# A planner with its first transfers in the order of use and newly searched rank lists: a two-layer conditioned transformer on one Trainium2 core

## What is computed

```python
ada = (silu(cond) @ Wada.T + bada).reshape(8, 1, 6, 256)
gamma1, gamma2, scale1, scale2, shift1, shift2 = [ada[:, :, i, :] for i in range(6)]
x = x + attn0(ln(x) * (scale1 + 1) + shift1) * gamma1        # 16 heads of 16, cosine-normed q and k
x = x + (gelu((ln(x) * (scale2 + 1) + shift2) @ Wfc1.T + bfc1) @ Wfc2.T + bfc2) * gamma2
h = rms(x) * ln1_w * (1 + cond @ tw1.T)
x = x + attn1(rope(h @ Wq.T), rope(h @ Wk.T), h @ Wv.T) @ Wo.T     # 8 query heads of 32, one k/v head
h = rms(x) * ln2_w * (1 + cond @ tw2.T)
x = x + (silu(h @ Wg.T) * (h @ Wu.T)) @ Wd.T
```

## Time and profile before

| what | value |
|---|---|
| three runs | 308.78, 309.8, 311.77 us; median 309.8 us |
| profiled execution | 313.7 us, of which the span from first to last instruction is 311.6 us |
| mean granted TensorE clock | 0.967 of full |
| PE busy | 291.3 us of the span (93%), `warm` products included |
| DVE, ACT, POOL busy | 215.4, 205.5, 153.9 us |

### The profile page before, as it was taken

How to read it: one execution, slowest core, us unless ns; L and a number is a source line. 1 busy time by engine, 2 the same in 40 slices (tenths; PEclk the granted TensorE clock), 3 DMA queues, 4 the chain that set the end, 5 groups by cost and what they waited for, 6 DMA issues and landing times.

```text
span 311.6 us, 7095 instructions
## 1 busy us (share of the span) xinstructions
PE 291.3 (93%) x2412; PEld 244.5 (78%) x2412; DVE 215.4 (69%) x527; ACT 205.5 (66%) x698; POOL 153.9 (49%) x289
## 2 busy tenths in 40 slices
PE   7999979898879989978999999999999999999996
PEld 7879767666757768865987787899888988888985
DVE  4884599979496999988859787576445875463431
ACT  3574399999975998987889865737772342662210
POOL 3658687385976955797424456521424321222000
PEclk9795899999986999999999999999999999999999
DMA  6999532002010010000002000000000000000000
GB/s 185 243 299 331 150 104 97 8 1 70 0 36 0 16 54 3 1 3 0 2 0 69 1 3 0 2 2 17 18 3 2 0 8 28 1 2 25 12 2 34
DMA packets 14035, 14.28 MB, mean 46 GB/s; under 512 B 1568, under 2 KB 12960, under 8 KB 14000
## 3 DMA queue, kind: packets, MB, share of 16 engines
q1 hardware_dynamic: 14000, 13.83, 14.7%
HBM read 12.76 MB, written 1.06 MB: 44 GB/s over the span
## 4 chain that ended last, share of the span: by engine, by line
PE 56%; DVE 19%; POOL 12%; issue 6%; ACT 4%; DMA 1%; SPq 1%; DVEq 0%; POOLq 0%
PE ps_shared L1570 16%; PE ps_shared L1377 8%; PE ps_shared L1379 7%; PE ps_shared L1378 7%; PE ps_shared L1543 4%; DVE z L1265 3%; PE ps_output L1524 2%; PE ps_shared L1508 2%; ACT z L990 2%; PE ps_scores L1497 2%; DVE neg_max L1276 2%; PE ps_scores L1407 2%; PE ps_shared L1413 2%; DMA X<-in_x 1%; PE ps_shared L1397 1%
## 5 line engine op out<-in xcount | busy, mean ns | idle before, releaser
L990 ACT ACTIVATE z<-z,neg_max 128x128 f32<-128x128 f32 x128 | 49.9, 404 | 5.8 <-DVE neg_max L1276 5.8
L830 POOL TENSOR_TENSOR h_lo<-xn,h_hi 128x256 fp32r<-128x256 f32 x32 | 24.1, 756 | 35.5 <-ACT h_hi L954 31.6
L1570 PE MATMUL ps_shared<-Wfc2T,g_h 128*128 128x256 f32 x128 | 33.0, 403 | 0.5 <-DVE g_h L1335 0.5
L1508 PE MATMUL ps_shared<-ident,z 128*128 128x128 f32 x192 | 29.4, 276 | 4.1 <-ACT z L990 1.9
L994 ACT ACTIVATE z<-ps_scores,neg_max 128x128 f32<-128x128 f32 x64 | 22.6, 368 | 14.7 <-DVE neg_max L1282 14.4
L1010 ACT ACTIVATE probsT<-ps_shared 128x512 f32<-128x512 f32 x48 | 28.8, 599 | 4.6 <-PE ps_shared L1508 3.6
L884 POOL TENSOR_TENSOR z<-z,row_inv 128x512 f32<-128x512 f32 x16 | 16.6, 1040 | 28.7 <-DVE row_inv L1290 28.5
L1570 PE MATMUL ps_shared<-WdT,g_h 128*128 128x256 f32 x128 | 30.1, 381 | 0.5 <-DVE g_h L1348 0.5
L1046 ACT ACTIVATE g_a<-ps_shared 128x256 f32<-128x256 f32 x32 | 12.4, 386 | 25.8 <-PE ps_shared L1379 21.4
L1508 PEld LDWEIGHTS ps_shared<-ident,z 128*128 128x128 f32 x192 | 22.0, 140 | 8.7 <-issue 6.3
L1570 PEld LDWEIGHTS ps_shared<-Wfc2T,g_h 128*128 128x128 f32 x128 | 24.2, 199 | 5.0 <-issue 1.0
(11 more groups left out here) (164 smaller groups left out, 884.7 us busy)
## 6 DMA issues: line engine op xcount, KB each, us to landing
gamma<-gamma_scratch SPq DMA_DIRECT2D x8, 256.0 KB, 3.6
stage<-in_Wada SPq DMA_DIRECT2D x6, 256.0 KB, 4.9
X<-in_x SPq DMA_DIRECT2D x4, 256.0 KB, 3.8
stage<-in_Wqkv SPq DMA_DIRECT2D x4, 256.0 KB, 5.5
Wfc2T<-in_Wfc SPq DMA_DIRECT2D x1, 1024.0 KB, 8.1
stage<-in_Wfc SPq DMA_DIRECT2D x4, 256.0 KB, 5.2
WdT<-in_Wd SPq DMA_DIRECT2D x1, 1024.0 KB, 6.7
stage<-in_Wg SPq DMA_DIRECT2D x4, 256.0 KB, 2.6
```

Source lines behind the costliest of these rows:

```text
L830: pool.tensor_tensor(h_lo[:, m, :, j * P:(j + 1) * P], h_full[:, m, j, :, :], h_hi[:, m, :, j * P:(j + 1) * P].bitcast(F32), ALU.subtract) ...
L990: ins = act.activation(z[:, d, u, :], z[:, d, u, :], ACT.Exp, bias=neg_max[:, d, u:u + 1], accum_out=head_sum[:, n % 2, t, u, b:b + 1])
L1508: ins = pe.transpose(bank[:, u * P:(u + 1) * P], z[:, G % DEEP, u, :], ident[:, :])
L1570: ins = pe.matmul(psum[b][:, 0:C], g_h[:, f, j * P:(j + 1) * P], WT1[name][:, f, :], start=(f == 0), stop=(f == FT - 1))
```

## The change

1. The ten first DMA steps get an order by hand (`FIRST`): their ranks are replaced by their places in that list, less a million. `pos` and `columns` are issued by ACT, ahead of its first instruction, and no longer by SP.
2. All rank lists (`GROUP_US`, `ATT_BASE`, `MLP_BASE`, `CHUNK_SHIFT`, `MLP_SPAN`, `SHIFT`) have new values.
3. Some planned durations are set anew, and `fc1` and `gate_up` may in the plan not run before the third-last gate is done. No instruction waits for more than before by it.
4. The clock model counts a `modulate` as 0.15 of its time, measures recent work over a sliding stretch when it decides on a `warm`, and keeps a high clock at a busy share of 0.6 (0.55 before).

No arithmetic, tile or semaphore of a step is changed; but all five orders, the banks and the number and places of the `warm` products come out of the planner anew.

```diff
+FIRST = ([("load_x", 0)] + [("load", c) for c in range(5)] + [("load_small",), ("load_x", 1), ("load", 5), ("load", 6),
+                                                              ("load_x", 2)])
...
-ATT_BASE = [-4247.0, -1474.0, -480.5, -362.5, 1970.0, -2902.0, 13.0, 1115.0]
-MLP_BASE = [936.0, 5182.0, -1432.5, 1460.0, -2095.0, -3629.5, 3064.0, -4297.5]
+ATT_BASE = [-4846.0, -3968.5, -278.0, -1190.0, 872.5, -4610.5, -4606.5, -699.0]
+MLP_BASE = [-999.0, 5454.0, -3139.0, 1474.0, -3599.0, -3395.0, 8429.5, -748.5]
...
-WARM_US, WARM_KEEP, WARM_RAISE = 0.22, 0.55, 0.95
+WARM_US, WARM_KEEP, WARM_RAISE = 0.22, 0.6, 0.95
+ACTIVITY = {"modulate": 0.15}
...
-    add(("cond_tanh",), "ACT", 2.8, at=-9)
+    add(("cond_tanh",), "ACT", 3.6, at=-9)
...
-        add(("load_x", p), "SP", 0.95, [],
+        add(("load_x", p), "SP", 0.95 if p else 1.7, [],
             at=-4.5 if p == 0 else ATT_BASE[2 * p - p % 2] + START - 20)
...
-                add(("qk_root", n), "Pool", 3.1, [("qk_sum", n)], at=a)
-                add(("qk_scale", n), "DVE", 0.75, [("qk_root", n)], at=a)
+                add(("qk_root", n), "Pool", 3.35, [("qk_sum", n)], at=a)
+                add(("qk_scale", n), "DVE", 0.95, [("qk_root", n)], at=a)
...
-            add(key, "PE", 1.51, [("norm_low", "m", 2 * r + 1), ("weight_low", w_ready)] + o[-1:], "shared", at=a)
+            add(key, "PE", 1.51, [("norm_low", "m", 2 * r + 1), ("weight_low", w_ready)] + o[-1:] + done[-3:-2], "shared", at=a)
...
-    return {k: (*v[:5], round(v[5] - path[k], 3)) for k, v in steps.items()}
+    return {k: (*v[:5], FIRST.index(k) - 1e6 if k in FIRST else round(v[5] - path[k], 3)) for k, v in steps.items()}
...
-                    us *= slow
-                    active += us
+                    us *= slow
+                    share = ACTIVITY.get(k[0], 1.0)
+                    active += us * share
+                    worked.append((now, now + us, share))
...
-                    if active < share * (now - window * CLOCK_WINDOW):
+                    since = now - CLOCK_WINDOW
+                    while worked and worked[0][1] <= since:
+                        worked.pop(0)
+                    recent = sum(w * (t1 - max(t0, since)) for t0, t1, w in worked)
+                    if recent < (WARM_KEEP if slow == 1.0 else WARM_RAISE) * min(now, CLOCK_WINDOW):
...
-            sp.dma_start(cols[:, 2 * N_SEQ:V0 + N_VEC], columns).then_inc(vec_loaded, 16)
-            sp.dma_start(pos_i[:, :], pos).then_inc(pos_loaded, 16)
...
         @block.scalar
         def _(act):
+            act.dma_start(cols[:, 2 * N_SEQ:V0 + N_VEC], columns).then_inc(vec_loaded, 16)
+            act.dma_start(pos_i[:, :], pos).then_inc(pos_loaded, 16)
```

More of the change, by code:

```diff
@@ L90 @@
+MLP_SPAN = [308.5, 2292.5]
 SHIFT = {
[L91 to L110, removed]
+    'warm': 900.0, 'angles': -2777.5, 'attn_copy': 1801.0, 'cond_silu': 3034.0, 'cond_tanh': 1647.0, 'down':
@@ new lines @@
+    4045.5, 'exp': 4489.0, 'fc1': -6047.5, 'gamma_load': -3148.0, 'gamma_store': 4661.0, 'gate': 3951.0,
+    'gate_up': 1799.5, 'gelu': -3728.5, 'gelu_in': 1876.0, 'gelu_inner': 1673.0, 'head_clip': -3201.5,
+    'head_exp': 2007.5, 'inv_copy': 2629.0, 'inv_spread': -1819.5, 'inv_turn': -3087.5, 'k_copy': 863.0,
+    'k_turn': 614.5, 'load': -2701.0, 'load_small': -2304.5, 'load_whole': 3744.0, 'load_x': -1760.5,
+    'mask_add': 437.0, 'modulate': 4093.5, 'modulated': -2328.0, 'norm_apply': -7684.5, 'norm_high':
@@ new lines @@
+    -4248.5, 'norm_low': 781.5, 'norm_mod': 1141.0, 'norm_probs': 963.0, 'norm_root': 11715.5, 'norm_stats':
+    -5932.5, 'norm_turn': 3032.5, 'probs_copy': -804.5, 'probs_turn': -897.0, 'project': -47.0, 'q_copy':
+    1206.0, 'q_turn': 3594.0, 'qk1_copy': 5525.5, 'qk1_turn': -10405.0, 'qk_copy': -2275.0, 'qk_high':
+    -2592.0, 'qk_low': -1220.5, 'qk_product': -4856.0, 'qk_root': 5555.0, 'qk_scale': 823.0, 'qk_square':
+    -4021.5, 'qk_sum': 919.5, 'qkv1_copy': -2814.5, 'qkv1_product': 3649.5, 'residual': -3156.0,
@@ new lines @@
+    'residual_add': 2346.5, 'rope': 6780.5, 'row_inverse': 3661.0, 'row_max': -4169.5, 'scores': 106.5,
+    'sines': 1611.5, 'store': 4409.0, 'sum_inverse': -6044.0, 'tanh': 3731.5, 'v_copy': -3365.0,
+    'v_product': -1368.0, 'values': -2796.5, 'weight_high': -579.5, 'weight_low': 2782.0, ('norm_stats',
+    'a'): -816.5, ('norm_stats', 'm'): 135.5, ('norm_root', 'a'): -619.5, ('norm_root', 'm'): -624.5,
+    ('norm_apply', 'a'): -3353.5, ('norm_apply', 'm'): 690.0, ('norm_turn', 'a'): -3449.0, ('norm_turn',
@@ L424, in make_orders, with clock @@
     plan, events, now, left = {}, [], 0.0, len(steps)
-    window, active, slow = 0, 0.0, 2.0
+    window, active, slow, worked = 0, 0.0, 2.0, []
+    def clock(now):
+        nonlocal window, active, slow
+        while now >= (window + 1) * CLOCK_WINDOW:
+            slow = 1.0 if active > 0.85 * CLOCK_WINDOW else 2.0 if active < 0.45 * CLOCK_WINDOW else slow
+            window, active = window + 1, 0.0
     warmed, n_pe = 0, sum(v[0] == "PE" for v in steps.values())
@@ L447, in make_orders @@
                 if e == "PE":
[L449 to L451 removed]
+                    clock(now)
                     us *= slow
[L453 removed]
+                    share = ACTIVITY.get(k[0], 1.0)
+                    active += us * share
+                    worked.append((now, now + us, share))
                 events.append((now + us, 0, k))
@@ L467, in make_orders @@
                         active += WARM_US * slow
+                        worked.append((now, now + WARM_US * slow, 1.0))
                         events.append((now + WARM_US * slow, 2, ("warm",)))
```

23 lines of the change are left out of this document (10 added, 13 removed).

## The result

The changed kernel takes 317.08 us (median of 4 runs, 316.31 to 317.96) against 310.5 us for the kernel before beside it: ratio 1.0211, 95% interval 1.0175 to 1.0246. It is slower by some 6.6 us, where 303.5 was forecast, in a range of 296 to 312.

A forecast was written before the change was run, and what follows sets the result against it. It saw a late start, a stretch nearly ACT's (40 to 88 us) and PE's block from 152 us. Terms 2.0 + 3.7 + 1.6 - 1.0 = 6.3 us, read from the profiled 313.7, taken off the median 309.8: 303.5, range 296 to 312.

The forecast's parts named there:

- First transfers: Start of the kernel: X of pair 0 loaded first brings the first `qk_product` forward, a gain of 2.0 us, lower end 0.
- `columns` and `pos` on ACT: Ahead of ACT's table load: `cond_tanh` some 0.8 us later, nothing on the path; without cover at most 0.8 us lost.
- The clock in the first 40 us: PE's chain from 24.22 us to `q_turn`: full clock removes its wait behind PE's queue, a gain of 3.7 us.
- the third stretch: Third low-clock stretch, 6.54 us of real work at half clock, 3.3 us too many; half taken as gain, 1.6 us.
- More `warm` products: PE before 40 us: 5 to 10 more pairs, half covered by waits, 1.0 us lost; ends 0 and 9.6 us.
- New ranks, planned durations and the gate condition: Reordering bounded by PE's idle 12.4 us from 40 to 152 us; entered as 0, ends +6 and -6 us.
- The slower one: Rival, PE's list from 14 to 34 us: added `warm` products stand before real work, 315.5 us; chance 0.13.
- The moved stretches: Rival: low-clock stretches move to new gaps between 40 and 152 us instead of going, 308.3 us; chance 0.28.
- the third rival: New lists also remove half of PE's 12.4 us idle from 40 to 152 us, 297.3 us; chance 0.17.
- The signs named in advance: Trace marks: right if first `exp` at 32 to 34 us; wrong if over 3 us at 0.50 after 14 us.

## Why the prediction was wrong, step by step

- *First transfers, 2.0 us.* X of pair 0 was issued at 0.71 us and there 2.9 us later, as said. The first product came at 12.88 us instead of 13.75: 0.9 us, at the low clock, so that the pass of six ended at 15.8, before at 15.4. The range of the term held this; its size was wrong. The weights came even earlier than priced (first `modulate` at 5.34 us, before at 7.88), but from there to the first product it took 7.5 us and not the 5.9 that I carried over. What I got wrong outright is the sentence that pair 1 "is wanted only by the second round's products". Who wants a tile is to be read from the list of the engine that reads it: pair 1's statistics stand on DVE ahead of pair 0's `norm_apply`. In the old lists that cost 4.8 us. In the changed ones the same wait is 2.04 us, at 14.00, and does no harm: the next step that PE needs, `qk_copy`, waits for PE until 15.85 anyway.
- *`columns` and `pos` on ACT, nothing on the path.* True for `modulate`; but `pos` landed 3.3 us after its issue (before, 1.9), the `angles` on DVE wait for it until 4.52 us, and `norm_stats` of pair 0, whose X was there by 3.6, stands behind them and runs at 5.78.
- *The clock in the first 40 us, 3.7 us, and the third stretch, 1.6 us.* In both, the changed kernel did not do what I expected: its plan puts in fewer `warm` steps, not more, and the clock fell in more places. The price itself holds for the execution from which it was read: the kernel before, held at full clock, takes 309.28 us, 4.4 less than the profiled 313.7, where the two terms came to 5.3. `q_turn` then ends 3.2 us earlier (31.5 against 34.7) and the first `exp` comes 2.2 us earlier, so the working of the step was right at its place; what failed is the sentence "Applied to 309.8 the sum gives 303.5". Over its median the kernel before gains 0.7 us (0 to 1.4 by the interval), and its own two executions at 1.00, without any added step, took 308.74 and 308.77. The profiled execution had a mean clock of 0.967; of the runs beside the experiments those at 0.983 or more took 308.5 to 311.3 us, most of them under 310.5, those at 0.972 and 0.978 took 310.8 to 313.0, and the three at 0.967 took 312.6, 312.6 and 313.8. A mean of 0.983 is what half a clock for some 10 us of 308 makes, an estimate, so the median execution has about half of the profiled one's 19.4 us. Which half is not shown, as no trace of one was kept. A gain that is read from a stretch which the median run does not have cannot be taken off the median.
- *More `warm` products, -1.0 us.* The sign of the count was wrong: 41, before 78. I had read only that `modulate` counts for less, which asks for more of them; the sliding stretch beside it asks for far fewer, as the run with the old rule (99) shows.
- *New ranks, planned durations and the gate condition, 0, with 6 us to either side.* This is the step that failed: a term without a row was put at nothing, and here is most of the result. Three parts are measured: the place of the first `row_max` behind `qk_sum`, with the splits beside it on POOL (2.7 us), the missing `warm` steps of the term above (2.3 us, 3.6 together), and 3.4 us that no single move brought back. For the last the prediction gave the wrong bound: it said that from 152 to 280 us "another order gains nothing", which is so, and took that for no risk. A stretch with PE at 127.1 of 128 us can only lose by a new order. PE now idles 3.4 us more in it, 2.4 of them in place of real work. The idle time there is 4.3 to 4.4 us in the changed kernel and in every run that keeps its lists there, whatever their clock or their first `exp`, and 0.9 to 1.1 us in the kernel before and its variants, other than the one with more work on POOL. That is the size of what is left; no run took it away, so that it is the whole of it is not shown. Nor is it shown how the loss divides between the ranks, the durations and the gate condition: with the ranks alone put back the kernel is 13 us slower still, and neither of the other two was put back alone.
- *The rivals.* The slower one had 0.13 and was ascribed to `warm` products in front of real work; its time comes nearest (315.5), but the mechanism is another, as there are fewer of them. The moved stretches (0.28) did happen, at 43 and 101 us instead of 92, without the gain that I put beside them. Against the third rival the text says that POOL is above 70% too; from 88 to 104 us it is 69%, which changes nothing. The signs named in advance were clear: a stretch at 0.50 behind 14 us, the first `exp` at 43.8 instead of 32 to 34, PE's block with gaps.

## What to carry to other kernels

On in-order engines a step that waits is a wait for everything in the list behind it; before a transfer or a step is moved, look up on each engine what stands behind its first reader, not who needs its data. A searched order is a fit to one set of durations and rules: change any of them and price the whole order as new, with a loss on the side where the bounding engine is already full, and compare the lengths of the plans first, which takes no chip. And before a gain is taken off a median, ask whether the median run has the stretch from which it was read.

## What the runs showed of the hardware

DVE's small operations can take six times as long beside POOL's: `qk_fl`, 128x32, was 1.17 us instead of 0.19 during the three splits that took 4.17 us together. The second `qk_rot`, 128x128, took 0.82 us instead of 0.28 in the rows above. In the changed kernel DVE is busy 10.8 us longer with the same instructions, nearly all of it in operations that touch SBUF alone: `xn` without a mean went from 7.0 to 9.5 us for its sixteen, `qk_n` from 9.0 to 10.7 for its eight. Rows of one line of the changed kernel, then of the kernel before, min/median/max in ns:

```profile
L1166 DVE TENSOR_SCALAR xn<-X,rstd x16: 343/515/1121, 112.6 to 288.3; 128x256 f32<-128x256 f32 x16
```
```profile
L1154 DVE TENSOR_SCALAR xn<-X,rstd x16: 343/352/820, 106.4 to 283.7; 128x256 f32<-128x256 f32 x16
```

The Trainium skill (SBUF — State Buffer, section SBUF: two separate sides) says that DVE and GpSimd share a pair of ports, and that an operation which needs it waits until the other engine's instruction has ended. The trace agrees: the operations that got longer have two SBUF tensors or go from SBUF to SBUF, and `qkT` copies out of PSUM stayed at 0.41 us. How much one of them loses depends on what meets it: `xn` lost 2.5 us here and 0.2 in the run with more work on POOL. A planner that gives each step one duration cannot see this.

The second surprise is the clock. The profiled execution before has 19.4 us at half speed and is 4.4 us longer than a kernel that runs at full clock throughout, where half of 19.4 would be 9.7, an estimate: more than half of it is hidden behind the other engines; the median execution is only 0.7 us longer. And whether the clock falls at a place is not settled by the order alone. The two versions with pair 1 early have the same lists up to the `values` step at 72 us. In the profiled execution of the one, PE ran at 0.50 from 23.5 to 33.0 us, and at 0.51 from 9.3 to 12.8; in that of the other at 1.00 in both.
